# One block at the start, a block's tail moved among its heads, and half of a pair's additions moved to another engine

## The reference

```python
x = x + _L0_attn_a_ref(_layernorm(x), ...)   # linear attention
x = x + _L0_ffn_ref(_layernorm(x), ...)      # routed experts, top 2 of 8
x = x + _L0_attn_b_ref(_layernorm(x), ...)   # full softmax attention, 16 heads of 8
x = x + _L0_ffn_ref(_layernorm(x), ...)
x = x + _L1_attn_a_ref(_layernorm(x), ...)   # causal attention, latent values of 64
x = x + _L1_ffn_ref(_layernorm(x), ...)      # best of 8 experts
x = x + _L1_attn_b_ref(_layernorm(x), ...)
x = x + _L1_ffn_ref(_layernorm(x), ...)
```

```python
# linear attention: no softmax, one 8 x 8 state for each head
q = elu(x @ Wq.T + bq) + 1;  k = elu(x @ Wk.T + bk) + 1;  v = x @ Wv.T + bv
kv = einsum('bhtd,bhte->bhde', k, v)
y = einsum('bhtd,bhde->bhte', q, kv) / (einsum('bhtd,bhd->bht', q, k.sum(2)) + 1e-6)
y @ Wc.T + bc
# full attention
probs = softmax(einsum('bqhd,bkhd->bhqk', q * SCALE, k))
out = einsum('bhqk,bkhd->bqhd', probs, v);  out @ Wo.T + bo
# causal attention: the same under a lower triangle, 1024 x 1024 for each head
att = softmax(where(causal, einsum('bthl,bshl->bhts', qc, k) * SCALE, -inf))
y = einsum('bhts,bshl->bthl', att, v);  y @ Wo + bo
```

## Time and profile before

| what | us |
|---|---|
| time, median of 3 runs | 3124.42 (3123.14 to 3127.61) |
| the profiled execution, own time | 3126.77 |
| its span in the trace | 3125.0 |
| busy in the span: PE / PEld | 2524.0 (81%) / 1116.2 |
| busy in the span: DVE / ACT / POOL | 2393.8 (77%) / 1900.3 / 1248.3 |
| stretch 0 to 42 us (load, first batch): PE / DVE / ACT / POOL busy | 14.8 / 23.3 / 6.9 / 9.9 |
| stretch 990 to 1051 (last heads and tail): the same | 47.1 / 28.4 / 40.9 / 25.8 |
| stretch 1950 to 1996 (last pair): the same | 33.4 / 8.6 / 23.1 / 40.1 |

### The profile page before, as it was taken

One profiled execution on the slowest core, in us unless ns is written; L12 is line 12 of the kernel. 1 busy time (PEld: TensorE's weight loads), 2 busy tenths in 40 slices (PEclk: granted clock), 3 DMA queues, 4 the chain that ended last, 5 costly groups with the idle time before them and its releaser, 6 DMA issues. The chain is left out here.

```text
span 3125.0 us, 47232 instructions
## 1 busy us (share of the span) xinstructions
PE 2524.0 (81%) x13300; PEld 1116.2 (36%) x13300; DVE 2393.8 (77%) x4041; ACT 1900.3 (61%) x3798; POOL 1248.3 (40%) x1678
## 2 busy tenths in 40 slices
PE   5897799999999799979999999886655555555565
PEld 4644222222222444424444444475521011111465
DVE  6667788888888366878888888463389999999723
ACT  2212588888888310336666666234459999999644
POOL 1114533333333301549999999605560000000055
PEclk8899899999999899979999999987889999999788
DMA  3002322222232200822222223441221111110013
GB/s 97 1 0 64 102 74 76 77 72 74 77 114 73 63 1 1 288 88 86 86 86 86 86 86 104 139 157 43 61 99 35 31 33 32 32 33 27 28 38 85
DMA packets 192543, 221.77 MB, mean 71 GB/s; under 512 B 55760, under 2 KB 122064, under 8 KB 192000
## 3 DMA queue, kind: packets, MB, share of 16 engines
q1 hardware_dynamic: 160560, 192.76, 19.3%
q0 software_dynamic: 30240, 25.04, 3.3%
q10 hardware_dynamic: 1520, 1.31, 0.2%
HBM read 134.58 MB, written 83.76 MB: 70 GB/s over the span
## 5 line engine op out<-in xcount | busy, mean ns | idle before, releaser
L1320 DVE TENSOR_REDUCE neg_max<-ps 128x1 f32<-128x1024 f32 x512 | 602.5, 1220 | 93.7 <-PE ps L1213 86.9
L1293 ACT ACTIVATE prob<-ps 128x512 f32<-128x512 f32 x1024 | 556.3, 601 | 88.2 <-PE ps L1227 79.5
L1751 POOL TENSOR_TENSOR acc<-acc,prob 128x512 f32<-128x512 f32 (+3 forms) x640 | 579.4, 949 | 32.7 <-PE ps L1566 32.7
L2298 DVE TENSOR_REDUCE neg_max<-ps 128x1 f32<-128x1024 f32 x512 | 579.5, 1211 | 2.8 <-PE ps L2284 2.8
L2327 ACT ACTIVATE ps<-ps,neg_max 128x1024 f32<-128x1024 f32 x512 | 557.1, 1088 | 3.3 <-DVE neg_max L2298 3.3
L2284 PE MATMUL ps<-k_stack,q_stack 128*128 128x512 bf16 x1024 | 317.9, 393 | 266.0 <-ACT ps L2327 261.5
L1679 ACT ACTIVATE prob<-ps 128x512 f32<-128x512 f32 (+3 forms) x640 | 270.9, 473 | 215.5 <-PE ps L1554 158.9
L1720 DVE TENSOR_REDUCE neg_max<-ps 128x1 f32<-128x512 f32 (+7 forms) x512 | 388.0, 758 | 17.5
L1227 PE MATMUL ps<-q_stack,k_stack 128*128 128x512 bf16 x1024 | 311.2, 385 | 2.8 <-ACT prob L1293 2.0
L1237 PE MATMUL ps<-prob,v 128*32 128x512 f32 x2048 | 280.5, 620 | 0.9 <-ACT prob L1293 0.7
L2284 PEld LDWEIGHTS ps<-k_stack,q_stack 128*128 128x128 bf16 x1024 | 58.8, 98 | 524.8 <-ACT ps L2327 521.0
(11 more groups left out here) (322 smaller groups left out, 4001.3 us busy)
## 6 DMA issues: line engine op xcount, KB each, us to landing
q_stack<-q_parts SPq DMA_DIRECT2D x576, 48.0 KB
k_stack<-k_parts SPq DMA_DIRECT2D x576, 48.0 KB
o_quads<-o_out SPq DMA_DIRECT2D x64, 256.0 KB, 4.5
v<-v_wide SPq DMA_DIRECT2D x32, 512.0 KB
o_pairs<-o_out SPq DMA_DIRECT2D x64, 256.0 KB, 5.9
num<-o_pairs SPq DMA_DIRECT2D x8, 2048.0 KB, 8.1
q_parts<-parts SPq DMA_DIRECT2D x24, 384.0 KB, 2.6
k_parts<-parts SPq DMA_DIRECT2D x24, 384.0 KB, 2.8
```

The lines of the kernel that those rows point to most:

```text
L1293: nc.scalar.activation(prob[:, m % RING, :], ps[:, bank(m), :], ACT.Exp).then_inc(exped.sem, 1)
L1320: nc.vector.tensor_reduce(neg_max[:, i.slot(2), m:m + 1], ps[:, first:first + 2, :].rearrange("p b n -> p (b n)"), AX.X, ALU.max, negate=T ...
L1751: nc.gpsimd.tensor_tensor(sums, sums, weights(j, u, h), ALU.add).then_inc(added.sem, 1)
L2298: nc.vector.tensor_reduce(neg_max[:, i.slot(2), qt:qt + 1], ps[:, 2 * (qt % 4):2 * (qt % 4) + 2, :], AX.XY, ALU.max, negate=True).then_inc ...
```

## The change

1. **Load and linear attention become one block.** `load_phase` is gone. SP loads groups 0 and 1 of x, then six weights, then groups 4 to 7, then the bias row; ACT issues groups 2 and 3. DVE takes the statistics of groups 0 and 1, works the mean and deviation of these 8 tiles out (`FIRST`) and normalizes them; the other 24 tiles' statistics are spread between the steps of batch 0, and a second tail (`REST`) follows before batch 1 is normalized. ACT takes two square roots, and so changes its table twice more than in a plain run of exponentials. POOL makes the constants in the same block and adds the bias to x when the bias row is there.
2. **Full attention.** The inversion is cut in four pieces of 96x128 (an addition and a reciprocal each), put behind the reduces of heads 55 to 58. POOL adds the bias to the groups of x at heads 16 to 23, stores the reciprocals in step 59, reads them back in step 60 and weighs two groups in each of steps 61, 62 and 63.
3. **Causal attention.** Of the last pair DVE makes the ten additions of h=1 after its thirds, and POOL only those of h=0. Two semaphores count them, and `sum_up` waits for both.

```diff
+                load_x(sp, 0)
+                load_x(sp, 1)
+                for dst, src in weights:
+                    sp.dma_start(dst, src).then_inc(weights_loaded, 16)
+                for g in range(4, GROUPS):
+                    load_x(sp, g)
+                for dst, src in biases:
+                    sp.dma_start(dst, src).then_inc(biases_loaded, 16)
...
+                load_x(act, 2)
+                load_x(act, 3)
+                act.wait_ge(eps_set, 1)
+                first_deviation(act, FIRST, 1)
+                nc.scalar.activation(exp_warm[:, 0:1], S.eps[:], ACT.Exp)
...
                 for s in (0, 1):
                     evacuate(0, s)
                     exponentials(0, s)
+                first_deviation(act, REST, 2)
+                nc.scalar.activation(exp_warm[:, 1:2], S.eps[:], ACT.Exp)
...
+                for g in (0, 1):
+                    dve.wait_ge(x_loaded[g], 16)
+                    first_stats = group_stats(nc, S, g)
+                first_mean_and_rstd(dve, first_stats, FIRST, 1)
                 normalize(0, 0)
                 normalize(0, 1)
-                for s in (0, 1):
-                    add_biases(0, s)
-                    normalize(1, s)
-                    take_exponentials(0, s)
+                dve.wait_ge(weights_loaded, 16 * len(weights))
+                nc.vector.tensor_scalar(S.a0_bq1[:], S.a0_bq[:], 1.0, None, ALU.add).then_inc(bq1_made, 1)
+                add_biases(0, 0)
+                for g in (2, 3, 4):
+                    dve.wait_ge(x_loaded[g], 16)
+                    group_stats(nc, S, g)
+                dve.wait_ge(bq1_made, 1)
+                take_exponentials(0, 0)
+                for g in (5, 6, 7):
+                    dve.wait_ge(x_loaded[g], 16)
+                    rest_stats = group_stats(nc, S, g)
+                add_biases(0, 1)
+                first_mean_and_rstd(dve, rest_stats, REST, 2)
+                normalize(1, 0)
+                take_exponentials(0, 1)
+                normalize(1, 1)
...
+    INVERT = early.FROM + 3
+    INVERTED = INVERT + early.PIECES
...
+                if 0 <= n - INVERT < early.PIECES:
+                    early.invert(dve, n - INVERT)
...
-            early.invert(dve)
...
-            early.store_reciprocals(pool)
-            for g in range(early.GROUPS_DONE):
-                early.load_reciprocals(pool, g)
-            for g in range(GROUPS):
-                early.bias(pool, g)
-                if 0 <= g - 1 < early.GROUPS_DONE:
-                    early.weigh(pool, g - 1)
+                if 0 <= c - H < GROUPS:
+                    early.bias(pool, c - H)
+                if c == INVERTED:
+                    early.store_reciprocals(pool)
+                if c == INVERTED + 1:
+                    for g in range(early.GROUPS_DONE):
+                        early.load_reciprocals(pool, g)
+                if 0 <= c - INVERTED - 2 < early.GROUPS_DONE // 2:
+                    for g in (2 * (c - INVERTED - 2), 2 * (c - INVERTED - 2) + 1):
+                        early.weigh(pool, g)
...
             def sum_up(j):
-                added.wait(pe, j.times(ADDS, ADDS - 1))
+                for h in (0, 1):
+                    wait_for_added(pe, j, NU - FIRST - 1, h)
...
             run(dve, step)
             early.invert(dve)
+            for u in range(FIRST, NU):
+                add(dve, nc.vector, Head(0, NP - 1), u, 1)
...
                     for u in range(FIRST, NU):
                         for h in (0, 1):
-                            add(i - 2, u, h)
+                            if h == 0 or n - 2 < NP - 1:
+                                add(pool, nc.gpsimd, i - 2, u, h)
```

More of the change, by code:

```diff
@@ new lines, in norm_stats, with mean_and_rstd, deviation @@
+def norm_stats(nc, sb, sem, S, name=""):
+    tmp = sb(name + "bn_tmp", [P, 4, TILES])
+    stats_made, chain, var_ready, std_ready = [sem(name + n) for n in "stats_made norm_chain var_ready std_ready".split()]
+    links = Shared()
+    links.chain = None
+    def mean_and_rstd(dve, last_stats, tiles=slice(0, TILES), turn=1):
+        last_stats.then_inc(stats_made, 1)
+        dve.wait_ge(stats_made, turn)
+        if turn == 1:
+            links.chain = Chain(dve, chain)
+        stats_tail(nc, dve, links.chain, S.st, tmp, S.mean, S.rstd, var_ready, std_ready, tiles, turn)
+    def deviation(act, tiles=slice(0, TILES), turn=1):
@@ L212, in deviation @@
         nc.scalar.activation(S.act_warm[:], S.eps[:], ACT.Sqrt)
-        act.wait_ge(var_ready, 1)
-        nc.scalar.activation(tmp[:, 1], tmp[:, 2], ACT.Sqrt, bias=S.eps[:], scale=1.0 / D).then_inc(std_ready, 1)
+        act.wait_ge(var_ready, turn)
+        nc.scalar.activation(tmp[:, 1, tiles], tmp[:, 2, tiles], ACT.Sqrt, bias=S.eps[:], scale=1.0 / D).then_inc(std_ready, 1)
     return mean_and_rstd, deviation
@@ L228, in keep_turning, with linear_attention @@
         nc.tensor.matmul(S.ps[:, bank, 0:2 * P], S.ident[:], S.a0_wkv[:], start=True, stop=True)
-def linear_attention(nc, S):
+def linear_attention(nc, S, x_in, weights, biases):
     ctx, sb, sem, steps = scope(nc)
@@ L329, in outputs @@
                     op.then_inc(o_mm.sem, 1)
-                for s in (0, 1):
-                    transpose(0, s)
-                    inputs(0, s)
+                pe.wait_ge(made, IDENT_MADE)
+                transpose(0, 0)
+                pe.wait_ge(weights_loaded, 16 * len(weights))
+                inputs(0, 0)
+                transpose(0, 1)
+                inputs(0, 1)
                 accumulate(0)
@@ L392, in _ @@
                 x_biased.open(pool)
+                links = make_constants(nc, S, pool, made)
+                assert links == ALL_MADE, links
+                pool.wait_ge(biases_loaded, 16 * len(biases))
                 with pool.Fori(0, GROUPS) as g:
@@ L1472, in bank, with added_for, wait_for_added, add @@
         return S2 + (len(turns) * c + turns.index(what)) % RING2
+    def added_for(j, h):
+        return added if j.c < NP - 1 else (last_added, also_added)[h]
+    def wait_for_added(eng, j, n, h):
+        if j.c < NP - 1:
+            added.wait(eng, j.times(ADDS, 2 * n + h))
+        else:
+            added_for(j, h).wait(eng, n)
+    def add(eng, op_of, j, u, h):
+        kt, c = units[u]
+        exped.wait(eng, j.times(2 * NU, 2 * u + h))
+        if kt == 1:
+            pv_mm.wait(eng, j.times(2 * NU, 2 * c + h))
+        else:
+            wait_for_added(eng, j, units.index((kt - 1, c)) - FIRST, h)
+        sums = acc[:, j.slot(2), h, c, offset(u):GROUP]
+        op_of.tensor_tensor(sums, sums, weights(j, u, h), ALU.add).then_inc(added_for(j, h).sem, 1)
     def wait_for_bank(pe, what, c):
@@ L1740, in split_shift @@
                                         ALU.subtract).then_inc(split.sem, 1)
-            def add(j, u, h):
-                kt, c = units[u]
-                exped.wait(pool, j.times(2 * NU, 2 * u + h))
-                if kt == 1:
-                    pv_mm.wait(pool, j.times(2 * NU, 2 * c + h))
-                else:
-                    last = units.index((kt - 1, c)) - FIRST
-                    added.wait(pool, j.times(ADDS, 2 * last + h))
-                sums = acc[:, j.slot(2), h, c, offset(u):GROUP]
-                nc.gpsimd.tensor_tensor(sums, sums, weights(j, u, h), ALU.add).then_inc(added.sem, 1)
             def step(i, n):
```

162 lines of the change are left out of this document (71 added, 91 removed).

## The result

The changed kernel takes 3113.07 us, median of 7 runs (3103.51 to 3117.56), and the one before, in as many, 3125.6 (3123.14 to 3127.61). The ratio is 0.9957 (0.9944 to 0.9970): 12.5 to 13.4 us less. I had predicted 3109, in a range of 3100 to 3117. The execution profiled after is the shortest of the seven: 3103.51, span 3101.8. So its trace gains 23.2 us, and 10 of them are of that execution alone; where they lie is the first thing to find.

The account below looks back on a forecast made before the run. No engine bounded the start, where engines hand one another small pieces; POOL set the ends of full attention and causal attention's last pair. Terms −5.5 − 10.1 + 4.0 + 1.5 − 6.0 = −16.1 from 3124.42 gave 3108.3, predicted 3109, range 3100 to 3117.

Parts of the forecast that it names:

- the start: Load and linear attention up to batch 0's state: state taken at 36.5 instead of 42.04, −5.5 us, bounds −10.4 to −1.
- the DMA queue: POOL's queue near head 62: six reads ahead of head 62's `load_low` cost +1.5 us, bounds 0 to 4.
- one of my own signs: Heads 60 to 63: forecast wrong if PE waits for POOL or its queue for more than 4 us.
- The block's end: Full attention behind the last head: block ends with PE's drain and SP's store, not POOL, −10.1 us.
- The pieces: Four inversion pieces on DVE among full attention's reduces: 0.95 to 1.0 us each, +4.0, bounds 0 to 5.1.
- The last pair: Causal attention's last pair: DVE takes ten additions, PE's wait of 5.86 us shrinks, −6.0 us, bounds −6.8 to −1.
- the heads pay more: Rival, full attention's heads: pieces at 1.27, queue at 4, some wait on POOL, 9 for 5.5; time 3112; chance 0.13.
- the start gains little: Rival, at the start: x lands late, second table change stands in the way; start −1, time 3113; chance 0.12.
- The slower one: Rival, heads 61 to 63: POOL's DMA queue jams and each of three heads stands still; time 3131; chance 0.03.
- Pieces hide: Rival, full attention and start: pieces cost +1 and the start gives −8; time 3103; chance 0.11.

Follow-up runs that it names:

- e2: Only the full-attention part (inversion in pieces, POOL's moved work) added to the kernel before: ratio 0.9999 (0.9988 to 1.0010) to the kernel before.
- e6: Changed kernel with POOL's six reads issued in step 62, weighings behind head 63, and inversion in 20 small steps: ratio 0.9923 (0.9911 to 0.9936) to the kernel before.

## Why the prediction was right, and where not

The time, 3113.07, is in the range, and 0.13% above the 3109. The gain was forecast as 16.1 us and is 12.5 to 13.4. Three of the five terms were right. Two were off: the start gave 1.2 more, and the DMA queue cost 4.2 more. By one of my own signs I was wrong: PE waited 4.24 us for POOL's queue at head 62, and I had set 4.

- **Start, −5.5.** Measured −6.7. The first transposition came at 9.24, not 10.7: group 1 landed at 5.57, hardly later than 5.38, so the 1.4 that I had added for shared queues weren't needed. The path to the state was longer by 5.0, near the 4.9 worked out, but not made of the same: neither L446 escaped POOL (1.36 and 1.42, so the −1.5 didn't come), the 24 statistics took 4.8 (I had 5.2) and the second tail 2.8 (26.95 to 29.75; I had 3.5), and 2.6 of these 7.6 lay in gaps. That the sum came out so near is luck in part.
- **The block's end, −10.1.** Measured −10.1, in each trace that keeps the change's reads or has them by SP.
- **The pieces, +4.0.** Measured +3.4, 0.86 for each; a piece hid 0.41 of its 1.27, the first gap, as said.
- **The DMA queue, +1.5, bounds 0 to 4.** Measured +5.7, outside the bounds; this is the step that failed. Its slack was wrong twice. PE wants the low-order parts not at the split but at the start of its own step, 2.3 us ahead of it (985.74 − 4.24 = 981.5, with the split at 983.76). And I had taken 2.8 for the landing from the row of q_low, where the last k_low, issued at 989.02, took this long already in the kernel before:

```profile
DMA to landing us min/median/max: 4.0/4.0/4.0
```

It landed at 993.0, PE wanted it at 994.2, and the slack was 1.2 and not 4.0. Behind the reads it was issued 3.4 later against the split and took 6.0 to land, 2.0 more: 3.4 + 2.0 − 1.2 is 4.2, the 4.24 seen. On top come the 1.4 of PE's products at the low clock behind the wait, which I hadn't counted; e2 shows the same (a wait of 4.14, then 1.3 more at a granted clock of 0.54).
- **The last pair, −6.0.** Measured −6.15. That DVE is ahead of the exponentials held (it waited 11.12 us). That neither engine stands for more than one operation of the other didn't: DVE's ten additions took from 0.29 to 6.96 us, not 0.7 to 1.6. It cost nothing in seven of ten profiles, since DVE caught up, and about 2 us in the other three, where DVE's additions went first.

The rivals: that the heads pay more is what came true, as to the heads (9.0 against my 5.5), and its time of 3112 is near. I had given it 0.13. The start made up 1.2 of its loss. The closest time of all, 3113, is that of the rival in which the start gains little, by luck alone: the start gained 6.7 and not 1. The slower one, a jam over three heads, didn't come: one head stood still. "Pieces hide" was false as the change has them, and true of steps cut to the size of the gaps (e6).

## What to carry to other kernels

When a large transfer is put ahead of a small one that an engine waits for, find the moment when the engine wants the small one (its own first instruction on it, not a marker nearby), and put the large one behind it or in another issuer's queue: the same bytes cost 5.7 us ahead of it, 0.7 to 1.5 behind it, where they met another small one, and 0.4 or nothing in SP's queue. An engine that is made to stand can cost more than the wait, when its clock is low behind it. Work moved into the waits of an engine that is nearly full costs what it is longer than each wait; cut to the waits' size, it was all but free. And cut a trace at a few fixed instructions in several profiles before believing a difference: of the 23 us between the two first profiles, 14 were the change.

## What the runs showed of the hardware

- PE's granted clock is low for a longer or shorter time in the start and the small layers from one execution to the next: 0.95 and 0.93 on average over the same 296 us of the same program, which took 286.8 and 293.4 us from the state to head 0.
- After PE had stood for 4.24 us at head 62, its next eleven products ran at a granted clock of 0.52 and took 3.19 us; a little earlier eleven such had taken 1.84, at 1.00.
- DVE and POOL both adding in SBUF don't share: in seven profiles a DVE addition of 128x384 stood for 6.96 to 6.99 us beside POOL's unbroken ones, and in three DVE's went first (0.68 to 1.00 each) and POOL's took 1.05, 1.17 and 0.63 in place of 0.74, 0.74 and 0.47. The Trainium skill ("SBUF — State Buffer") has an exclusive lock for such a pair of operations, held for an instruction; that the side which comes back to back can keep the other out for eight of its instructions is what the 6.96 show beyond it.
- Six small transfers behind 1.5 MB in POOL's queue landed after 5.3 to 6.1 us, and beside the end of the same bytes in SP's queue after 2.6 to 4.6.
- The kernel before took 3123.2 us on one chip and 3075 to 3078 on three (and 3125.6 in the first comparison), with nearly all of the difference behind causal attention.
